# Experts' single-block tiles five tiles apart, weight pieces two tiles earlier, and a new order of two lists in the first attention's prologue

## What is computed

```
x = x + L0_xattn(ctx, layernorm(x))       # 4 heads of 64, layernorms and rms norms inside, 77 keys of ctx as well
x = x + L0_ffn(layernorm(x))              # 8 experts, top 2: relu(x w1 + b1) w2 + b2, F = 1024
x = x + L1_xattn(layernorm(x), ctx)       # 16 heads of 16, 77 keys
x = x + L1_ffn(layernorm(x))              # 8 experts, top 2: (silu(x w1) * (x w2)) w3, H = 512
```

## Time and profile before

| what | value |
|---|---|
| time, median of 3 runs | 1573.96 us (1572.23 to 1576.97) |
| the profiled execution | 1573.92 us |
| its span, first to last instruction | 1572.2 us |
| mean granted TensorE clock | 0.917 of full speed |
| PE busy | 1430.4 us, 91% of the span |
| DVE, ACT, POOL busy | 1036.2, 829.4, 685.5 us |

### The profile page before, as it was taken

One profiled execution on the slowest core, in us unless ns is written; L12 is line 12 of the kernel. 1 busy time (PEld: TensorE's weight loads), 2 busy tenths in 40 slices (PEclk: granted clock), 3 DMA queues, 4 the chain that ended last, 5 costly groups with the idle time before them and its releaser, 6 DMA issues. The chain is left out here.

```text
span 1572.2 us, 35956 instructions
## 1 busy us (share of the span) xinstructions
PE 1430.4 (91%) x12426; PEld 1048.7 (67%) x12426; DVE 1036.2 (66%) x1991; ACT 829.4 (53%) x1513; POOL 685.5 (44%) x525
## 2 busy tenths in 40 slices
PE   8799999999986699999999978999978499999996
PEld 2433333333355589989899966777758389999885
DVE  5678888888768645555555427888958755455443
ACT  2678888887743245556555524667744032222221
POOL 2522212211110254555545425777752246666554
PEclk6899999999975699999999996999995599999998
DMA  5332333232238365556577433000016274334553
GB/s 166 111 108 82 102 115 132 82 115 74 81 105 299 110 181 132 145 141 161 130 200 192 103 71 107 23 6 28 29 30 240 86 226 68 62 66 68 109 136 49
DMA packets 114589, 175.77 MB, mean 112 GB/s; under 512 B 18992, under 2 KB 76644, under 8 KB 114148
## 3 DMA queue, kind: packets, MB, share of 16 engines
q1 hardware_dynamic: 84375, 132.93, 25.6%
q0 software_dynamic: 27264, 37.82, 13.7%
q10 hardware_dynamic: 2791, 2.84, 0.6%
HBM read 106.34 MB, written 67.23 MB: 110 GB/s over the span
## 5 line engine op out<-in xcount | busy, mean ns | idle before, releaser
L1601 PE MATMUL e_ph<-e_zTt,weights_a 128*128 128x256 f16 x3072 | 350.4, 275 | 2.0 <-DVE e_zTt L1695 2.0
L1601 PEld LDWEIGHTS e_ph<-e_zTt,weights_a 128*128 x3072 | 302.6, 99 | 39.4 <-issue 2.5
L1655 ACT ACTIVATE e_h<-e_ph,e_b 128x256 f32<-128x256 f32 (+1 forms) x312 | 123.6, 453 | 185.9 <-PE e_ph L1601 185.6
L1551 POOL DMA_INDIRECT token_rows<-e_ysb,slot_token x71 | 128.4, 1808 | 172.2 <-DVE e_ysb L1734 158.0
L1615 PE MATMUL e_pyt<-weights_b,e_hh 128*128 x1136 | 192.7, 273 | 1.2 <-DVE e_ysb L1734 1.1
L1541 POOL DMA_INDIRECT gathered<-token_parts,slot_token x138 | 141.6, 1026 | 54.4 <-issue 46.7
L1717 DVE TENSOR_TENSOR e_hl<-e_h,e_hh 128x512 f16<-128x512 f32 x142 | 94.8, 690 | 103.5 <-ACT e_hh L1666 103.5
L680 PE MATMUL middle_banks<-probs,v 128*64 128x512 f32 (+1 forms) x576 | 152.9, 613 | 8.7 <-ACT raw_o L811 7.9
L1551 POOL DMA_INDIRECT out_dram<-e_ysb,slot_token x71 | 113.2, 1594 | 106.0 <-DVE e_ysb L1737 75.1
L935 DVE TENSOR_TENSOR acc<-acc,probs 128x1024 f32<-128x1024 f32 (+1 forms) x112 | 138.6, 1238 | 27.4 <-ACT probs L804 24.8
L1615 PE MATMUL e_pyt<-weights_b,e_hl 128*128 x568 | 154.8, 273 | 0.0
(11 more groups left out here) (274 smaller groups left out, 2805.6 us busy)
## 6 DMA issues: line engine op xcount, KB each, us to landing
weight_parts<-w_split SPq DMA_DIRECT2D x32, 512.0 KB, 3.4
weights_a<-weight_parts SPq DMA_DIRECT2D x16, 1024.0 KB, 7.4
x_sb<-weight_parts SPq DMA_DIRECT2D x14, 1024.0 KB, 6.9
x_sb<-in_u SPq DMA_DIRECT2D x24, 512.0 KB, 4.9
weight_parts<-x_sb SPq DMA_DIRECT2D x24, 512.0 KB, 3.4
w_raw<-in_w1T SPq DMA_DIRECT2D x16, 512.0 KB, 4.4
w_raw<-in_w2T SPq DMA_DIRECT2D x16, 512.0 KB, 4.8
weights_b<-weight_parts SPq DMA_DIRECT2D x8, 1024.0 KB, 9.5
```

Of the source, the lines that this page charges most:

```text
L1551: pool.indirect_dma_start(g.rows[layer], at, ysb[:, s, c, :], None, compute_op=ALU.add).then_inc(sto[s], 16)
L1601: last = pe.matmul(out[:, f, :], weights_up(i, e, wp, k, per[i] * q + f), zTs[:, s, 2 * zp + k, 0:cols[i] * P], start=(n == 0), stop=(n == 5))
L1655: last = act.activation(parted(hidden(h32, n), i)[:, f, :], parted(ph[:, bank_of(i, q)], i)[:, f, :], ACT.Relu, bias=b1[:, bass.ds(e, 1), ...
```

## The change

Four edits. `single` now marks tiles 8, 13, 18, 23, 28, 33 and 38 in place of 26, 28, 30, 32, 34, 36 and 38, in both layers. The pieces of layer 1's weights are handled from tile 2 to 25 in place of 4 to 27. In the prologue of the first attention, ACT's list has `high` first, and DVE's list has `low` and `norm` ahead of `ln_low` and `sums`.

```diff
@@ attention0, scalar @@
-            pipeline([(gain_and_shift, 0, 2), (squares, 1, 2), (high, 3, 0), (parts_out, 4, 0),
+            pipeline([(high, 3, 0), (gain_and_shift, 0, 2), (squares, 1, 2), (parts_out, 4, 0),
@@ attention0, vector @@
-            pipeline([(center, -1, 2), (ln_low, 0, 2), (sums, 1, 0), (low, 3, 0), (norm, 2, 0),
+            pipeline([(center, -1, 2), (low, 3, 0), (norm, 2, 0), (ln_low, 0, 2), (sums, 1, 0),
@@ constants @@
-SINGLES_FROM = 2 * PAIRS - NT
+APART = 5
+SINGLES_FROM = NT - 1 - APART * (NT - PAIRS - 1)
@@ experts @@
-    FIRST_PIECE = 4
+    FIRST_PIECE = 2
@@ experts @@
-    single = [i > SINGLES_FROM and (i - SINGLES_FROM) % 2 == 1 for i in range(NT)]
+    single = [i >= SINGLES_FROM and (i - SINGLES_FROM) % APART == 0 for i in range(NT)]
```

## The result

| | before | after |
|---|---|---|
| median of 14 runs each | 1571.92 us (1567.05 to 1576.97) | 1578.65 us (1573.21 to 1586.15) |
| the profiled execution, its span | 1573.92, 1572.2 us | 1578.52, 1576.8 us |

The ratio is 1.0049, 95% interval 1.0036 to 1.0063: the changed kernel is 7.7 us slower (5.7 to 9.9). 1577.9 was predicted, from a start of 1573.92, so a change of +4.0.

A forecast was written before the change was run, and what follows sets the result against it. PE, busy 39.86 of 40 us in a window of layer 0's experts, was taken as the bound. From 1573.92 us, -6.8 for singles, +4.85 for lists and +5.9 for the first piece gave 1577.9, range 1570.5 to 1583.5.

The forecast's parts named there:

- The three terms: Singles apart -6.8 us, the prologue's two lists +4.85, weight pieces two tiles earlier +5.9, added to 1573.92.
- Lists: Prologue of the first attention: the new order of ACT's and DVE's work costs +4.85 us, bounds +2.8 to +6.6.
- The closed chain: Prologue: each turn runs from norm through sums and POOL's power to the next norm, 4.45 us against 3.46.
- fit into the wait: Prologue: weight pieces that DVE makes in two steps were to fit in its wait for POOL's power.
- The rival of a falling clock: Prologue: PE waits each turn and its clock drops to 1.2 GHz, giving 1582.5 us; chance 8%.
- First piece: Start of layer 0's experts: ACT waits for the fetched piece, delaying tile 4's `up`; +5.9 us, bounds 0 to 7.8.
- the landing: Layer 0's experts: the first fetched weight piece arrives at 573.0 us, behind the last expert's weights.
- Singles: Layer 1's experts: singles five tiles apart gain 6.7 us, bounds 5.1 and 7.6; layer 0 adds 0.1.
- the 0.9 that I took off: Layer 1's singles: deduction for one more add ahead of the end and PE's remaining loads of two expert numbers.
- the 7.62: Layer 1's experts: us lost between the first and last single, against six turns of 12.52 us.
- 2.07 us to spare: Layer 1's experts: time a gather keeps with one single among pairs, so that no wait comes.
- the prediction's own sign: Layer 1's experts: the forecast would be wrong if PE's waits for gathered rows stay in the profile after.

The follow-up runs named there:

- experiments 7 and 8: Kernel before with only DVE's new prologue list, and with only ACT's: first center to first sum of the main loop 61.07 and 48.97 us.
- Experiment 6: Kernel before with both new prologue lists, and norm taking the power of the tile before: first center to first sum of the main loop 45.46 us.
- experiments 2: Kernel before with both new prologue lists and nothing else: ratio to the kernel before 1.0042, 6.6 us slower.
- Experiment 4: Changed kernel with the first two fetches of weight pieces issued ahead of the last three experts' weights: ratio to the kernel before 1.0022.
- Experiments 5 and 10: Kernel before with singles five tiles apart and PE's reads of expert numbers moved: ratio 0.9975; kernel before with only the reads moved: 0.9997.

## Why the prediction was right, and where it was not

The three terms had the right sign, and two of them were near their size; the gain of the singles was not. That the time itself lies within 0.8 us of the forecast is partly luck: the sum started at 1573.92, which is 2.0 above the median of the 14 runs of the kernel before, and it forecast a change of +4.0 where 7.7 was found.

**Lists: +4.85 predicted, +4.6 found** (means of center to sum: 46.89 in the four profiles with both lists as changed, 42.31 in the seven with neither). The closed chain is there link by link: from the norm at 54.53 on 0.73 to the gain product, 0.34 to `ln_low`, 0.33 to the sums, 0.97 to the power, 1.74 for it and 0.03 to the next norm, 4.14 in all. Two steps in it were wrong and cancelled nearly. The power took 1.74 in three of the seven turns and 2.02, which I had picked for all, in two. And the sentence that the weight pieces "fit into the wait" is wrong: the turn with the first piece takes 63.79 - 58.67 = 5.12, since the power beside it takes 2.72, and the power beside the second takes 2.55. That I priced DVE's chain alone was a gap: ACT's list is no bystander, as experiments 7 and 8 show, and the right sum came from the one combination in which the chain through POOL is longest. Experiment 6 sets the limit of this account: the chain is what the changed kernel waits for, but without the power 3.2 of the 4.6 us stay (45.46 - 42.31), in costs that I put at nothing.

The rival of a falling clock did not come true in the changed kernel, where the clock stays at 1.00 up to 80 us with PE busy 12.19 of the 21 us behind 59. So the rule of the Trainium skill that I weighed (page "TensorE: Matmul & The Clock Gate", section "A second HAM failure mode: psum-queue depth-cycling") did not decide here. That the clock can fall in this prologue, experiment 6 shows, and so do the profiles of experiments 2 and 4, which have the same lists (0.50 in 53 to 55 us and in 54 to 58). Their 45.81 and 47.75 are the shortest and the longest of the four, so what that costs stays open.

**First piece: +5.9 predicted, 4.1 to 8.9 found**, 6.8 in the mean of four profiles (386.75 less 379.98, the mean of the nine without it, fetches early apart). The mechanism is right, and the 5.90 from landing to `up` were 5.79. The mis-sized part is the landing: I put it 39.1 us after the first `up` of layer 0 (573.0 - 533.93), and in the four it was 41.5, 37.8, 38.6 and 40.7. The clock took 1.7 to 2.8, not 1.6. Experiment 4 shows the cause: an earlier fetch, and nothing is left.

**Singles: -6.7 predicted in layer 1, -0.9 found** (first to last `up` 295.99 in the mean of four with the singles apart and the reads in place, 297.68 in eight without the edit: -1.7; the end 21.02 against 20.25: +0.8). The step that failed is the 0.9 that I took off the 7.62 "for two things". The added end was 0.8 of it by itself. The other, "the places where PE loads two expert numbers at once stay", I had taken for a small rest; now each of the six pairs behind a single stops for 0.3 to 1.0 us, 3.7 in all by the steps from `up` to `up`, and late gathers still make 1.3, in places where I saw 2.07 us to spare. By the prediction's own sign, that waits for gathered rows stay, it was wrong here. Experiments 5 and 10 show that the reads are worth nothing without the singles apart, 2.8 us in layer 1's profile with them, and that both together give 3.9 of the 6.7 that I had promised for one (297.68 - 292.96, less 0.8 at the end).

By these landmarks the terms sum to 4.6 + 6.8 - 0.9 = 10.5 us; the medians say 7.7 (5.7 to 9.9). Executions of like clock agree with the medians: the three edits alone sum to 5.4 + 4.9 - 3.1 = 7.2 and 6.2 + 5.1 - 3.4 = 7.9 us. So the singles gave about 3 us in all, of which layer 1 shows 0.9. Two stretches that the sum leaves out point the same way: layer 0 from first to last `up` is 0.4 shorter with the singles apart (379.66 in two profiles, 380.07 in seven without, none of them with the piece at tile 2), and from the last `up` of layer 0 to the first of layer 1 it takes 338.3 in the mean of five profiles and 341.1 in nine without. Single profiles go from 336.9 to 344.3 there, in code that the edit doesn't touch, so whether the singles make that difference isn't shown.

Open also stays why a stop for two reads is 0.3 us at one single and 1.0 at another, and why some gathers are late among pairs.

## What to carry to other kernels

A loss that is read between two points of a trace is not the gain of moving its cause: ask which wait ends next at the same place, and price that from the new order, since two hidden costs (here late rows, and the reads of numbers) can each cover the other. When two engines' lists are reordered, follow the chain through both; either half alone can be worse than the two, as here. And work that stands in line for a transfer should be moved earlier only together with the transfer's issue: with the fetches early the same edit cost nothing.

## What the runs showed of the hardware

The input stage ran at one of two clocks, and the first center came at 40 or at 46 us, in executions of one and the same kernel: the changed one had 40.27 and, again, 46.06. Differences of a few us between two profiled executions say nothing until this is taken out.

A short operation of POOL was stretched by DVE's work beside it: the power of 8 columns took 2.72 us at 61.04, when DVE's product of a weight piece began at the same moment (61.03, 1.23 us long), 2.55 beside the second piece, 1.74 in four of the other six and 2.02 in two. The Trainium skill, page "SBUF — State Buffer", section "Who interferes with whom", says that a DVE instruction with two SBUF inputs contends with a GpSimd instruction that reads SBUF; the 0.98 us more than 1.74 agree with that.
